# Four similarity matmuls in a row, the naming of choices behind the batch maximum's column, and the entry list ahead of the shared sums, in a decoder layer with 160 experts

## The chip, the core and the metric

The kernel runs on one core of one Trainium2 chip. The metric is the device time of one execution in microseconds (us). A core has TensorE (PE; its weight loads are shown as PEld), VectorE (DVE), ScalarE (ACT), GpSimd (POOL) and SyncE (SP). They work through their own queues of instructions and wait for each other by semaphores. Transfers run on 16 DMA engines that all queues share.

## The reference

One post-norm decoder layer on x of (4, 512, 256): self-attention with 16 heads, a two-way attention to a context of the same size, and a feed-forward part with 160 routed experts (8 per token) and one shared expert. The part that the change touches:

```python
Sim = (hc @ w1)[:, :, None] + (hq @ w2)[:, None, :] + einsum('bid,bjd->bij', hc * w3, hq) + b_sim[0]
A = softmax(Sim, axis=2)
hq_hat = einsum('bij,bjd->bid', A, hq)
Batt = softmax(max(Sim, axis=2), axis=1)
hc_bar = einsum('bi,bid->bd', Batt, hc)
hcq = concatenate([hc, hq_hat, hc * hq_hat, hc * hc_bar], -1) @ W_qv + b_qv
x2 = layernorm(x1 + hcq)
probs = sigmoid(x2 @ router_w.T + expert_bias)
top_w, top_idx = top_k(probs, 8)          # weights divided by their sum, times 2.5
out = layernorm(x2 + routed experts + shared expert)
```

## The kernel before

The layer runs in four blocks, one behind the other: `attend` (self-attention), `mix` (two-way attention, norms, routing), `experts` and `combine`. The order of every engine's work is written out by hand; there is no scheduler. The change is in `mix`.

`mix` works batch by batch (B = 4), each of 512 tokens in TT = 4 tiles of 128, in five turns n = 0 to 4. Turn n does the two-way attention of batch n (`part_b`, n < 4), the routing of batch n - 1 (`part_c`, n > 0) and the projection of batch n + 1 (`part_a`, n < 3).

In a turn, TensorE forms four tiles of similarities into PSUM banks 4, 5, 2 and 3 (`SIMILAR`), 128 x 512 each. For tile i, VectorE takes the negative row maximum (`row_max`), ScalarE the exponential with the row sums (`exp_row`), VectorE the inverse (`invert_row`), ScalarE scales (`scale_row`), TensorE transposes the row of tiles (`turn_row`, banks 6 and 7) and ScalarE copies it out (`copy_row`). With all four there, TensorE multiplies with the context (`attended(0)`, `attended(1)`). Beside this the batch's own softmax runs: `u` from the row maxima, its maximum `um` turned into one row (L1020), the global maximum `g`, spread by a matmul (L1023), then `eb`, then the sums that give `W1` (L1533). The mixing matmuls (L1057, L1063) follow.

The routing of the batch before runs through the same turn on VectorE: `highest` (8 largest of 160), `strike`, `mark` (the mask; TensorE ranks it, `rank`, L949 and L951), `name` (the indices of the eight, and their weights, written into `rows`), `count_rows` (reads the ranks), `grow`, `put` and `places`, the last two for tiles 0 and 1 and later for tiles 2 and 3. Each `places` raises `rows_done`, and POOL then scatters the rows of those tiles to the DRAM tensor `row_pool` with one indirect DMA for each tile and choice, 32 for a batch (L1985). `name` must be done before, since its results are in the rows.

In turn 4 TensorE also computes the shared expert, whose output VectorE adds for one batch at a time (`add_shared`, L1251, two additions each). `list_entries` makes the list of experts and pages; SP stores it to DRAM (L864) and loads it back for every partition (L866); `fill_tables` turns it into the tables, and `tables_done` lets SP start the weight loads of the first five entries of the experts' ring (L1593). The first row loads of the experts wait in `rows_sent` until every scatter has landed.

Of the kernel before, what the change touches and what calls it, by code (L numbers as in the profile page):

```python
# [30 lines left out]
B, S, D = 4, 512, 256  # L31
DC = D // P
TT = S // P
# [73 lines left out]
def repeated(ap, at, count):  # L107

    shape = list(ap.shape)
    return ap.unsqueeze(at).broadcast_to(shape[:at] + [count] + shape[at:])  # L110
# [504 lines left out]
class Order:  # L615
# [6 lines left out]
    def do(self, ins):  # L622
        self.n += 1
        ins.then_inc(self.sem, 1)

    def sync(self, but=0):
        self.eng.wait_ge(self.sem, self.n - but)
# [123 lines left out]
def mix(nc, inputs, opening, ps, x, ctx_t, ctx_r, od, rows, place, dispatch, last_sent, tables, w, pool, listing, pool_filled, spent):  # L751
# [8 lines left out]
    with ExitStack() as ctx:  # L760
# [149 lines left out]
        def _(pe):  # L910
# [61 lines left out]
            def step(n, part_b, part_c, part_a):  # L972
# [16 lines left out]
                def similarity(i):  # L989
                    for c in range(DC):  # L990
                        if i == 0:
                            pe.wait_ge(x1t_done, n * DC + (c + 1))
                        last = nc.tensor.matmul(ps[:, SIMILAR[i]], ET[:, c, i * P:(i + 1) * P], CT[:, c],
                                                start=c == 0, stop=c == DC - 1)
                    last.then_inc(similar, 1)

                def turn_row(i):
                    pe.wait_ge(row_scaled, tile(i))
                    if i >= 2:
                        pe.wait_ge(at_done, tile(i - 2))  # L1000
                    for j in range(TT):
                        last = nc.tensor.transpose(ps[:, 6 + i % 2, j * P:(j + 1) * P],
                                                   A[:, i, j * P:(j + 1) * P], ident)
                    last.then_inc(row_turned, 1)

                similarity(0)
                similarity(1)
                for i in range(2, TT):
                    similarity(i)
                    turn_row(i - 2)  # L1010
                if n == 0:
                    pe.wait_ge(ones_set, 3)
                    pe.wait_ge(below_set, 1)
# [67 lines left out]
                if part_a:  # L1081
                    turn_x1(n + 1)
            run(pe, start, step)

        @block.scalar
# [90 lines left out]
        def _(dve):  # L1176
# [22 lines left out]
            def step(n, part_b, part_c, part_a):  # L1199
# [33 lines left out]
                def name():  # L1233
                    for t in range(TT):
                        do(nc.vector.max_index(names8[:, t], top[:, t], pr[:, t]))
                    sync(but=TT)
                    do(nc.vector.reciprocal(winv[:], tsum[:]))
                    sync()
                    do(nc.vector.tensor_scalar(winv[:], winv[:], ROUTED_SCALE, None, ALU.mult))
                    do(nc.vector.tensor_scalar(rows[:, n - 1, :, NAMES:ROW].bitcast(I32), names8[:], -1.0, float(EXPERTS),  # L1240
                                               ALU.mult, ALU.add))
                    sync()
                    do(nc.vector.tensor_tensor(rows[:, n - 1, :, D:CODES], top[:], repeated(winv[:], 2, TOP_K), ALU.mult))
                    o2.hold()

                def add_shared(b):

                    dve.wait_ge(shared_made, b + 1)
                    shared = two(SHARES[b])
                    for t in range(0, TT, 2):  # L1250
                        last = nc.vector.tensor_tensor(XS[b][:, t:t + 2], shared[:, t:t + 2], rows[:, b, t:t + 2, 0:D], ALU.add)  # L1251
                    last.then_inc(shared_added, 1)
# [223 lines left out]
                def row_max(i):  # L1476
                    dve.wait_ge(similar, tile(i))
                    nc.vector.tensor_reduce(nmax[:, i:i + 1], ps[:, SIMILAR[i]], AX, ALU.max, negate=True).then_inc(row_maxed, 1)

                def invert_row(i):  # L1480
                    dve.wait_ge(row_expd, tile(i))
                    nc.vector.reciprocal(rinv[:, i:i + 1], rsum[:, i:i + 1]).then_inc(row_inverted, 1)
# [13 lines left out]
                if part_b:  # L1496
                    row_max(2)
                    invert_row(1)
                if part_c:
                    name()  # L1500
                if part_b:
                    row_max(3)
                    invert_row(2)
                    dve.wait_ge(row_maxed, tile(TT - 1))
                    do1(nc.vector.scalar_tensor_tensor(u[:], nmax[:], -1.0, dots[:], ALU.mult, ALU.add))
                    sync1()
                    do1(nc.vector.tensor_scalar(u[:], u[:], bsim, None, ALU.add))
                    sync1()
                    nc.vector.tensor_reduce(um[:], u[:], AX, ALU.max).then_inc(um_done, 1)
                    invert_row(3)  # L1510
                    dve.wait_ge(um_turned, n + 1)
                    nc.vector.tensor_reduce(g[:], ps[0:1, 4, 0:P], AX, ALU.max).then_inc(g_done, 1)
# [39 lines left out]
                if part_a:  # L1552
                    use_x1(n + 1)
                if part_c and not part_b:
                    add_shared(0)
                    list_entries()
                    for b in range(1, B):
                        add_shared(b)
                    fill_tables()
                    dve.sem_inc(tables_done, 1)  # L1560
            run(dve, start, step)


# [484 lines left out]
```

## Time and profile before

| | us |
|---|---|
| median of 3 runs | 868.62 (867.92 to 869.75) |
| profiled execution, whole | 870.09 |
| profiled execution, span of the core's instructions | 868.3 |
| TensorE busy in it | 742.0 (85%) |
| VectorE busy | 494.8 (57%) |
| ScalarE busy | 386.5 (45%) |
| POOL busy | 365.2 (42%) |
| mean granted clock of TensorE | 0.942 of full |

In the trace `attend` ends at about 292 us, turn 0 of `mix` starts at 294.6, turns 1 to 3 at 343.9, 394.7 and 443.4, and the first matmul of the experts at 560.6. Rows of a timeline read: start, duration, engine, line, operation, output <- input, tile shape, count of merged instructions, and in brackets the idle time of the engine before them with what ended it. A record of TensorE is half of a matmul of this type, so four records are one tile of similarities. Between 292 and 560 us no engine is busy all the time: the share of busy time says little there, and the waits in brackets say what comes last.

### The profile page before, as it was taken

The numbers are of one execution on the slowest core, as the hardware profiler recorded it, in microseconds if no ns is written. First come the engines' busy times: TensorE is split into PE (matmuls) and PEld (weight loads), VectorE is DVE, ScalarE is ACT, GpSimd is POOL, SyncE is SP. The second block draws the span as 40 slices with busy tenths as digits, with TensorE's granted clock in tenths as the row PEclk, the third lists the DMA queues.
The fourth block names the chain that finished last, engine by engine and source line by source line (L and its number), as shares of the span: only waits on it lengthen the run. The fifth ranks groups of instructions, "written<-read, shape, count | busy, mean of one in ns | idle before, by whom it ended". The sixth has DMA issues, their size and how long they took to land. (4 is left out here: it accounts for less than half of the span.)

```text
span 868.3 us, 14833 instructions
## 1 busy us (share of the span) xinstructions
PE 742.0 (85%) x3782; PEld 491.9 (57%) x3782; DVE 494.8 (57%) x1316; ACT 386.5 (45%) x809; POOL 365.2 (42%) x368
## 2 busy tenths in 40 slices
PE   7979999999999898898979730199999999998495
PEld 3645444444445366474846520188887787786373
DVE  1577787777781416768687498134333433332287
ACT  2337677676766634326171300044554454454011
POOL 9400101011100200165775777357777775777200
PEclk9999999999999999999999975599999999999698
DMA  6799878788794220042332223699999999995695
GB/s 243 261 345 303 286 250 278 259 272 276 257 297 177 63 72 25 34 170 103 131 113 74 113 99 134 224 347 374 371 380 375 368 362 347 371 345 187 259 421 218
DMA packets 103699, 208.04 MB, mean 240 GB/s; under 512 B 26024, under 2 KB 51666, under 8 KB 97377
## 3 DMA queue, kind: packets, MB, share of 16 engines
q1 hardware_dynamic: 63008, 127.39, 42.7%
q10 hardware_dynamic: 25760, 44.89, 14.7%
q0 software_dynamic: 14880, 35.17, 11.1%
q8 instruction: 22, 0.36, 0.2%
q14 instruction: 29, 0.23, 0.1%
HBM read 118.35 MB, written 96.08 MB: 247 GB/s over the span
## 5 line engine op out<-in xcount | busy, mean ns | idle before, releaser
L1831 POOL DMA_INDIRECT contributions<-c_c,e_dest x182 | 177.2, 973 | 81.1 <-ACT c_c L1809 42.0
L1985 POOL DMA_INDIRECT row_pool<-rows,places x128 | 131.2, 1025 | 121.6 <-issue 104.1
L594 DVE TENSOR_REDUCE a_mx<-ps 128x2 f32<-128x1024 f32 x128 | 151.9, 1218 | 30.3 <-PE ps L368 30.2
L539 ACT ACTIVATE a_e<-ps 128x512 f32<-128x512 f32 x256 | 135.6, 600 | 62.0 <-PE ps L398 55.8
L1783 DVE COPY e_xt<-e_psx 128x256 f32<-128x256 f32 (+1 forms) x130 | 68.6, 530 | 99.7 <-PE e_psx L1715 94.4
L1729 PE MATMUL e_psg<-e_xt,e_w 128*128 128x64 f32 (+2 forms) x676 | 118.7, 308 | 1.5 <-issue 1.1
L1715 PE MATMUL e_psx<-m_c,rows 128*128 128x128 f32 x364 | 64.8, 285 | 57.3 <-DMA rows<-row_pool 57.2
L1802 ACT ACTIVATE e_g<-e_psg 128x128 f32<-128x128 f32 (+1 forms) x130 | 41.8, 321 | 160.4 <-PE e_psg L1729 133.7
L311 POOL MEMSET a_q<- 64x1024 f32 x32 | 30.3, 946 | 179.4 <-PE ps L398 178.3
L1740 PE MATMUL e_psy<-e_w,e_g 128*128 128x256 f32 (+1 forms) x442 | 104.1, 393 | 0.0
L398 PE MATMUL ps<-a_q,a_k 128*128 128x512 f32 x256 | 98.3, 450 | 5.7 <-ACT a_e L539 3.8
L1729 PEld LDWEIGHTS e_psg<-e_xt,e_w 128*128 128x128 f32 x676 | 95.4, 194 | 5.8 <-issue 2.0
L1715 PEld LDWEIGHTS e_psx<-m_c,rows 128*128 128x128 f32 x364 | 45.2, 144 | 84.1 <-DMA rows<-row_pool 60.5
L1809 ACT ACTIVATE c_c<-e_psy,e_weight 128x256 f32<-128x256 f32 x182 | 80.5, 473 | 27.5 <-PE e_psy L1740 23.6
L398 PEld LDWEIGHTS ps<-a_q,a_k 128*128 128x128 f32 x256 | 43.8, 189 | 80.0 <-ACT a_e L539 49.3
L368 PE MATMUL ps<-a_k,a_q 128*128 128x512 f32 x256 | 86.8, 420 | 0.0
L409 PE MATMUL ps<-a_e,a_v 128*32 128x512 f32 x512 | 68.2, 605 | 0.0
L1740 PEld LDWEIGHTS e_psy<-e_w,e_g 128*128 128x128 f32 (+1 forms) x442 | 57.2, 171 | 14.4 <-ACT c_c L1809 6.3
L368 PEld LDWEIGHTS ps<-a_k,a_q 128*128 128x128 f32 x256 | 47.6, 191 | 11.1 <-issue 3.6
L1755 DVE TENSOR_TENSOR e_same<-rows,t_expert 128x56 f32<-128x56 int32 x26 | 5.6, 216 | 59.8 <-DMA rows<-row_pool 59.8
L1904 PE MATMUL c_ps<-c_c,m_c 128*128 128x256 f32 x128 | 33.2, 405 | 6.5 <-DMA c_c<-contributions 6.2
L1028 PE MATMUL ps<-m_at,m_cr 128*128 128x512 f32 x64 | 34.5, 689 | 2.7 <-ACT m_at L1127 2.7
(287 smaller groups left out, 959.9 us busy)
## 6 DMA issues: line engine op xcount, KB each, us to landing
e_w<-w ACTq DMA_DIRECT2D x162, 256.0 KB
row_pool<-fill SPq DMA_DIRECT2D x32, 1260.0 KB, 7.4
rows<-row_pool SPq DMA_DIRECT2D x139, 140.0 KB
c_c<-contributions SPq DMA_DIRECT2D x16, 1024.0 KB, 17.5
a_k<-k_parts SPq DMA_DIRECT2D x64, 128.0 KB, 3.5
rows<-row_pool SPq DMA_DIRECT2D x78, 70.0 KB
a_q<-q_parts SPq DMA_DIRECT2D x32, 128.0 KB, 4.0
a_q<-q_parts SPq DMA_DIRECT2D x64, 64.0 KB, 3.4
```

The source lines that it names most:

```text
L368: last = nc.tensor.matmul(psS[:, pair, 1 - u], Q[:, at.slot, hh, qt * P:(qt + 1) * P], K[:, at.slot, hh], start=True, stop=True)
L398: nc.tensor.matmul(psT[:, BANK[k]], K[:, at.slot, hh, kt * P:(kt + 1) * P], Q[:, at.slot, hh], start=True, stop=True).then_inc(rescored, 1)
L409: last = nc.tensor.matmul(psO[rows], V[:, at.n // NG, kt, head * 2 * DH:(head + 1) * 2 * DH], E[:, kt * HG + hh], start=kt == 0, stop=kt = ...
L539: nc.scalar.activation(E[:, i], psT[:, BANK[i]], ACT.Exp, scale=DH ** -0.5).then_inc(expd, 1)
L594: nc.vector.tensor_reduce(mx[:, at.slot, qt, 2 * DH * pair::HALF], psS[:, pair], AX, ALU.max).then_inc(maxed, 1)
L1715: last = nc.tensor.transpose(ps_x(at, (c * n + k) * P, (c * n + k + 1) * P), X[:, page(at) + k, c * P:(c + 1) * P], ident)
L1729: last = nc.tensor.matmul(ps_g(f, n)[:, k * own:(k + 1) * own], W[:, place, c * INTER:(c + 1) * INTER], XT[:, f.slot % XT_RING, at0:at0 + ...
L1740: last = nc.tensor.matmul(ps_y(f, k)[i * high:(i + 1) * high], G[:, f.slot % XT_RING, k * P + i * high:k * P + (i + 1) * high], W[:, place ...
L1783: nc.vector.tensor_copy(XT[:, at.slot % XT_RING, 0:n], ps_x(at, 0, n)).then_inc(xt_done, 1)
L1809: nc.scalar.activation(Y[:, result(f) + k], ps_y(f, k), ACT.Copy, scale=weight[:, result(f) + k:result(f) + k + 1]).then_inc(y_done, 1)
L1831: nc.gpsimd.indirect_dma_start(out=contrib, out_offset=bass.IndirectOffsetOnAxis(ap=dest[:, result(f) + k:result(f) + k + 1], axis=0), in_ ...
L1985: nc.gpsimd.indirect_dma_start(out=pool, out_offset=bass.IndirectOffsetOnAxis(ap=place[:, b, t, k:k + 1], axis=0), in_=rows[:, b, t], in_o ...
```

## The change

Three things are moved and nothing is added or taken away.

1. TensorE runs all four `similarity(i)` before the first two `turn_row(i)`. Before, similarities 0, 1 and 2 came first, then `turn_row(0)`, `similarity(3)`, `turn_row(1)`.
2. VectorE runs `name()` behind the maximum `um` and ahead of `invert_row(3)`. Before, it stood between `invert_row(1)` and `row_max(3)`. In turn 4, without a `part_b`, its place stays the same.
3. In turn 4 `list_entries()` comes before all four `add_shared(b)`. Before, `add_shared(0)` stood ahead of it.

```diff
@@ TensorE, step @@
-                similarity(0)
-                similarity(1)
-                for i in range(2, TT):
+                for i in range(TT):
                     similarity(i)
-                    turn_row(i - 2)
+                for i in range(TT - 2):
+                    turn_row(i)
@@ VectorE, step @@
                 if part_b:
                     row_max(2)
                     invert_row(1)
-                if part_c:
-                    name()
                 if part_b:
                     row_max(3)
                     invert_row(2)
...
                     nc.vector.tensor_reduce(um[:], u[:], AX, ALU.max).then_inc(um_done, 1)
+                if part_c:
+                    name()
+                if part_b:
                     invert_row(3)
                     dve.wait_ge(um_turned, n + 1)
                     nc.vector.tensor_reduce(g[:], ps[0:1, 4, 0:P], AX, ALU.max).then_inc(g_done, 1)
@@ VectorE, step, turn 4 @@
                 if part_c and not part_b:
-                    add_shared(0)
                     list_entries()
-                    for b in range(1, B):
+                    for b in range(B):
                         add_shared(b)
```

Line numbers behind the first edit are one lower in the kernel after. TensorE in turn 0, from the first similarity (`m_ct,m_et`) to `attended(0)` (`m_at,m_cr`), before:

```order
L993 MATMUL ps<-m_ct,m_et 128x512 x6
L1002 MATMUL ps<-m_c,m_a 128x128 x4
L993 MATMUL ps<-m_ct,m_et 128x512 x2
L1002 MATMUL ps<-m_c,m_a 128x128 x4
L1020 MATMUL ps<-m_c,m_um 1x128
L1002 MATMUL ps<-m_c,m_a 128x128 x4
L1023 MATMUL ps<-m_g,m_ones 128x1
L1002 MATMUL ps<-m_c,m_a 128x128 x4
L1028 MATMUL ps<-m_at,m_cr 128x512 x4
```

and after:

```order
L993 MATMUL ps<-m_ct,m_et 128x512 x8
L1002 MATMUL ps<-m_c,m_a 128x128 x8
L1019 MATMUL ps<-m_c,m_um 1x128
L1002 MATMUL ps<-m_c,m_a 128x128 x4
L1022 MATMUL ps<-m_g,m_ones 128x1
L1002 MATMUL ps<-m_c,m_a 128x128 x4
L1027 MATMUL ps<-m_at,m_cr 128x512 x4
```

The two matmuls of the fourth similarity moved ahead of the first turned row (`m_a`); in turns 1 to 3 the ranking stands between the second turned row and `m_um` in both. VectorE in turns 1 to 3, from the mask to the global maximum, before:

```order
L1230 TENSOR_TENSOR m_mask<-m_prob,m_rep 128x640
L1231 TENSOR_SCALAR m_tsum<-m_tsum 128x4
L1478 TENSOR_REDUCE m_nmax<-ps 128x1
L1482 RECIPROCAL m_rinv<-m_rsum 128x1
L1235 MAX_INDEX m_names<-m_top,m_prob 128x8 x4
...
L1243 TENSOR_TENSOR rows<-m_top,m_winv 128x4x8
L1478 TENSOR_REDUCE m_nmax<-ps 128x1
L1482 RECIPROCAL m_rinv<-m_rsum 128x1
L1505 SCALAR_TENSOR_TENSOR m_u<-m_nmax,m_dots 128x4
...
L1509 TENSOR_REDUCE m_um<-m_u 128x1
L1482 RECIPROCAL m_rinv<-m_rsum 128x1
L1512 TENSOR_REDUCE m_g<-ps 1x1
```

and after:

```order
L1477 TENSOR_REDUCE m_nmax<-ps 128x1
L1481 RECIPROCAL m_rinv<-m_rsum 128x1
L1477 TENSOR_REDUCE m_nmax<-ps 128x1
L1481 RECIPROCAL m_rinv<-m_rsum 128x1
L1502 SCALAR_TENSOR_TENSOR m_u<-m_nmax,m_dots 128x4
...
L1506 TENSOR_REDUCE m_um<-m_u 128x1
L1234 MAX_INDEX m_names<-m_top,m_prob 128x8 x4
...
L1242 TENSOR_TENSOR rows<-m_top,m_winv 128x4x8
L1481 RECIPROCAL m_rinv<-m_rsum 128x1
L1512 TENSOR_REDUCE m_g<-ps 1x1
```

The four index searches and the four small operations behind them (all of `name()`) now stand between `m_um` and the last inverse.

## Rows read from the trace of the kernel before

**Rows 1.** Timeline of POOL: scatters that had to wait, and the last.

```profile
396.06 0.97 POOL L1985 DMA_INDIRECT row_pool<-rows,places  x1 [9.38 <-ACT m_et L1101]
...
465.12 0.97 POOL L1985 DMA_INDIRECT row_pool<-rows,places  x1 [6.69 <-DVEq L1320]
...
508.58 1.02 POOL L1985 DMA_INDIRECT row_pool<-rows,places  x1 [1.14 <-DVEq L1320]
...
550.80 0.97 POOL L1985 DMA_INDIRECT row_pool<-rows,places  x1 [0.30 <-issue]
```

**Rows 2.** Timeline of TensorE in turn 1.

```profile
343.86 5.39 PE L993 MATMUL ps<-m_ct,m_et 128*128 128x512 f32 x12 [0.96 <-ACT m_et L1101]
...
351.02 0.66 PE L1002 MATMUL ps<-m_c,m_a 128*128 128x128 f32 x4 [1.77 <-ACT m_a L1123]
...
351.51 1.88 PE L993 MATMUL ps<-m_ct,m_et 128*128 128x512 f32 x4
...
354.36 0.44 PE L951 MATMUL ps<-m_mask,m_ones 128*128 128x160 bf16 x4
...
356.69 0.66 PE L1002 MATMUL ps<-m_c,m_a 128*128 128x128 f32 x4
...
358.04 5.40 PE L1028 MATMUL ps<-m_at,m_cr 128*128 128x512 f32 x8 [0.69 <-ACT m_at L1127]
```

**Rows 3.** Timeline of ScalarE in turn 1: copy 0, exponential 3, scaling 3.

```profile
352.33 0.59 ACT L1127 ACTIVATE m_at<-ps 128x512 f32<-128x512 f32 x1
...
354.16 0.69 ACT L1118 ACTIVATE m_a<-ps,m_nmax 128x512 f32<-128x512 f32 x1 [1.24 <-DVE m_nmax L1478]
...
355.93 0.71 ACT L1123 ACTIVATE m_a<-m_a,m_rinv 128x512 f32<-128x512 f32 x1
```

**Rows 4.** Timeline of VectorE in turn 1: first instruction of `name()`, maximum 3, inverse 3.

```profile
350.99 0.07 DVE L1235 MATCH_VALUE_LOAD m_names<-m_top,m_prob 128x8 f32 x1
...
353.43 0.69 DVE L1478 TENSOR_REDUCE m_nmax<-ps 128x1 f32<-128x512 f32 x1 [0.59 <-PE ps L993]
...
354.97 0.16 DVE L1482 RECIPROCAL m_rinv<-m_rsum 128x1 f32<-128x1 f32 x1 [0.19 <-ACT m_a L1118]
```

**Rows 5.** TensorE, turns 0 to 3; last a stretch (..., granted clock, DMA share, GB/s).

```profile
300.45 0.66 PE L1002 MATMUL ps<-m_c,m_a 128*128 128x128 f32 x4 [0.49 <-ACT m_a L1123]
...
365.20 3.68 PE L1028 MATMUL ps<-m_at,m_cr 128*128 128x512 f32 x8
...
408.66 3.70 PE L1028 MATMUL ps<-m_at,m_cr 128*128 128x512 f32 x8 [0.69 <-ACT m_at L1127]
...
457.62 5.36 PE L1028 MATMUL ps<-m_at,m_cr 128*128 128x512 f32 x8 [0.69 <-ACT m_at L1127]
...
360.00:362.00 2.00, 2.00 (x4) 0.73 (x3) 1.93 (x5) 0.00 (x0) 0.00 (x0) 0.50 0.00 0
```

**Rows 6.** Timeline of turn 2: `W1` on VectorE, and the first mixing matmul.

```profile
416.15 0.88 DVE L1533 SCALAR_TENSOR_TENSOR m_w<-m_wqv,m_hc 128x256 f32<-128x256 f32 x2
...
417.64 0.59 PE L1057 MATMUL ps<-m_x1b,m_c 128*128 128x256 f32 x2
```

**Rows 7.** Timeline of VectorE in turn 4: a shared sum, and the start of fill_tables.

```profile
534.68 1.28 DVE L1251 TENSOR_TENSOR m_x<-ps,rows 128x512 f32<-128x512 f32 x2
...
539.60 0.27 DVE L1446 CAST t_entry<-m_lists 128x64 int32<-128x64 f32 x1 [1.25 <-DMA m_lists<-listing]
```

**Rows 8.** SP's queue; landing of L1985's scatters; a stretch as in rows 5.

```profile
545.45 3.91 SPq L1593 DMA_DIRECT2D e_w<-w  x7
...
555.63 1.33 SPq L1604 DMA_DIRECT2D rows<-row_pool  x2
...
DMA to landing us min/median/max: 2.4/2.5/5.6
...
554.00:555.00 1.00, 0.00 (x0) 0.00 (x0) 0.00 (x0) 0.00 (x0) 0.00 (x0) 0.50 0.25 98
```

**Rows 9.** Timeline of TensorE in turn 4: the last four ranking matmuls.

```profile
497.48 0.74 PE L951 MATMUL ps<-m_mask,m_ones 128*128 128x160 bf16 x4
```

## What the change does to the time: the prediction

> **What bounds the kernel now.** I read the queue of POOL first, then worked back to what releases it. POOL sends the 128 row scatters of the routing, 32 for each batch, at a pitch of 1.28 us, and the experts cannot start before the last of them has landed [rows 1, 8]. The reader should look at the idle times in brackets. The third batch's scatters begin at 465.12 after 6.69 us of waiting for VectorE; the fourth batch's at 508.58 after 1.14 us more than the usual 0.30 gap would be, so again VectorE's release came last, with 1.14 us of slack behind it: POOL itself was free at 507.44 [rows 1]. So the end of the mixing stage is set by when VectorE publishes places in turn 4, and that by the chain of turns 0 to 3. (Turn n does the cross-attention of batch n and the routing of batch n-1.) Behind the scatters the expert stage is shifted as a whole, since all its row loads wait for them [rows 8]. One gate of POOL at 396.06 hangs on the end of turn 1 and moves with the chain [rows 1].
>
> Within a turn I then read TensorE. Similarities 0 to 2 run without a gap, 5.39 us for 12 records; then TensorE idles 1.77 us for the first scaled row, turns it, and only now runs the fourth similarity (1.88 us) [rows 2]. That late similarity is what the rest waits for: VectorE idles 0.59 us for it and takes its maximum at 353.43, ScalarE starts the last exponential at 354.16 after 1.24 us of idling, the last scaling runs at 355.93, the last row is turned at 356.69 and `attended` starts at 358.04 [rows 2 to 4]. From there on TensorE is busy without a gap up to the end of the mixing matmuls, so what is gained at 358.04 in one turn is passed to the next.
>
> **Similarity 3 ahead of the turned rows, with name() out of the way (turn 1, by its own rows).** Twelve records end at 349.25 (343.86 + 5.39). Four more at the pitch of 0.43 end at 351.0 instead of 353.39, inside the idle 1.77 us; the first turned row still starts at 351.02 [rows 2]. VectorE, with name() moved away, takes maximum 3 at 351.05 rather than 353.43, ready at 351.75. ScalarE cannot use all of these 2.4 us: it still has scaling 1 and the copy of turned row 0 ahead, which stands from 352.33 to 352.92, so exponential 3 runs at 352.8 to 353.6 rather than from 354.16 [rows 3]. Then scaling 2 (0.7) and copy 1 (0.6) fill it to 354.7.
>
> name() costs 352.84 - 350.99 = 1.85 us [rows 4]. It now starts behind the batch maximum's column, which follows maximum 3 and inverse 2 by 0.74 us: about 352.65. It ends at 354.5, and inverse 3, possible from 353.6, comes at 354.6 to 354.75. Queued behind name() are inverse 3, the global maximum `g`, count_rows and grow; scaling 3 on ScalarE and the spread matmul on TensorE wait for the first two. But ScalarE is itself not free before 354.7, so name() costs the chain at most 0.1 us. Scaling 3 runs at 354.8 instead of 355.93, the last row turns at 355.55 instead of 356.69, and `attended` starts at 356.9: **1.1 us earlier**. VectorE's own chain gains less, about 0.4 us: `g` at 354.75 and count_rows at 354.95 instead of 355.35 or so, since it holds the same work and only lost waits (0.59 for the maximum, less what it now waits for exponential 2). If ScalarE's cover were gone, name() would cost 0.9 us here (354.5 - 353.6).
>
> Turn 0 has no routing. There TensorE idles only 0.49 us ahead of turned row 0 [rows 5], so that row now goes behind 1.7 us of similarity and starts about 0.9 us later; copy 0 then sits in front of exponential 3 on ScalarE. Exponential 3 still comes 1.0 us earlier: **0.9 us**.
>
> Turn 3 is as turn 1: 1.1. Turn 2 is different, and here is what is late next: W1, which VectorE makes behind its first places, is ready at 417.03, and TensorE takes it up at 417.64 [rows 6]. With TensorE 1.1 us earlier and VectorE 0.4, the slack of 0.6 is used up: **1.0 us**. In turns 1 and 3 `attended` runs slower (below), so that slack is larger. Sum of the four turns: 0.9 + 1.1 + 1.0 + 1.1 = **4.1 us** at turn 4. The third batch's scatters start 0.9 + 1.1 + 1.0 + 0.4 = 3.4 us earlier; POOL is then free at 507.44 - 3.4 = 504.0 and VectorE releases the fourth at 508.58 - 4.1 = 504.5, so nothing is capped. The context load that SP issues after similarity 3 goes out up to 2.4 us earlier and is needed a whole turn later: nothing.
>
> **List entries ahead of the shared sums (turn 4).** One shared sum is two additions, 1.28 us as a row, 1.2 us in pitch [rows 7]. Moving the first behind the list brings the list to SP 1.2 us earlier. Its round trip through DRAM is now covered by four sums rather than three, the wait of 1.25 us ahead of fill_tables [rows 7] goes, and the tables are done 1.2 us earlier relative to the rest. That is not on the path by itself: the weight loads it releases (545.45) are through at about 554.3, long before the first expert matmul. What it can touch is the landing of the last scatter: a scatter lands in 2.5 us at the median, but the last, issued at 550.80, released the row loads only at 555.63, while seven weight loads held the DMA engines until 554.3 [rows 1, 8]. Lower bound 0 (the landing was slow for another reason), upper bound 555.6 - 550.8 - 2.5 = 2.3 us. If the scatter sits behind the loads it follows their end, 1.2 us. I take **1.0 us**, near that row. The Trainium skill, "DMA: Bandwidth & Descriptors" (its part on arbitration), says that each DMA engine goes round between its queues packet by packet. By that the scatter would not queue behind all of the loads and the gain would be nearer 0.6, the sum 0.4 us smaller; the profile's slow landing only shows that they disturb each other.
>
> **TensorE's clock, the cost that the diff doesn't show.** In turns 0, 1 and 3 the matmuls of `attended(0)` take 5.35 to 5.40 us, in turn 2 3.70, as `attended(1)` does in all four (3.68) [rows 2, 5]: the granted clock fell to 0.50 (1.2 GHz) at or just before them and they lost 1.7 us. What went before is a stretch of turned rows and small matmuls with gaps, 4.65 us long from the end of similarity 3 (353.39) to `attended` (358.04), and the same length in all four turns. The change takes 1.7 us of dense matmuls out of its front: from 351.0 to 356.9 it is 5.9 us long. Three falls in four at 4.65 us make the fourth likely at 5.9. Bounds: none of the falls (-5.1 us against now) and longer low stretches, which would catch the ranking too: its last four matmuls took 0.44 us at the full level and 0.74 in turn 4 at the low one, so its 14 would lose about 1.0 [rows 2, 9]. I take one more fall, in turn 2: **+1.7 us**.
>
> **Sum.** -4.1 - 1.0 + 1.7 = -3.4 us. Against the profiled execution (868.3 span, 870.1 with what lies around it) that is 866.7; it lies 1.5 us over the median of the timed runs, about one low-clock stretch, so that it may hold one more than a typical run. Taken from the median: 868.6 - 3.4 = **865.2 us**.
>
> **Rivals.**
> A. The clock falls as often as now: 868.6 - 5.1 = 863.5. For it: turn 2 got through 4.65 us with no fall. The Trainium skill, "TensorE: Matmul & The Clock Gate" (HAM oscillation), has the engine keep its full clock as long as it has no single long idle gap, and the change makes none; the trace disagrees, as the clock fell in turn 1 behind gaps of at most 1.8 us.
> B. The longer stretch brings the clock down before the ranking as well and in every turn: 4 x 1.7 + 3 x 1.0 = 9.8 us instead of 5.1, net -0.4: 868.2. Against it: the ranking of turn 1 still ran at the full level (0.44 us at 354.36), after that idle 1.77 us [rows 2].
> C. Slower: the same, and in two turns the low level also holds through `attended(1)`, another 1.7 us each: +3.0, 871.6. The place is the stretch in front of `attended(0)`; it decides from three more low stretches (5.1 us). For it speaks only that turn 4 shows long low stretches; against it, that `attended(0)` itself brought the clock back each time (its later part and all of `attended(1)` ran at the full level).
> D. The chain moves but POOL or the DMA takes it back: the list gains nothing, and name() in front of inverse 3 and of the places costs 0.5 us per turn, as if ScalarE had no other work ahead of scaling 3. Then -4.1 + 1.5 + 1.7 = -0.9: 867.7.
>
> **How the numbers follow.** Forecast 0.46, A 0.26 (with fewer falls than now in it), D 0.10, B 0.12, C 0.06. What can be told from no change is about 0.2% or 1.7 us: forecast and A are faster, and a third of D; B and the rest of D are the same, C slower. So faster 0.75, same 0.19, slower 0.06. The range reaches from A with 0.9 us of the list's upper bound (862.6) to B (868.2); outside are C and the rarest cases of A.
>
> **What would show it.** Right: 16 similarity records in a row; exponential 3 about 1.3 us nearer the first similarity; turned row 3 and `attended(0)` 1.1 us nearer; no idle time ahead of fill_tables; POOL's fourth batch starting 2 to 4 us earlier. Wrong on name(): ScalarE idle ahead of scaling 3 with VectorE as releaser. Wrong on the clock: `attended(0)` durations of 3.7 or over 5.4 in other turns than I said. Wrong on the list: the last scatter still takes 4.8 us until the row loads.

## The result, and the profile after

| | before | after |
|---|---|---|
| median | 868.22 us (866.27 to 869.75, 6 runs) | 861.7 us (861.31 to 864.59, 6 runs) |
| ratio | | 0.9913 [0.9888, 0.9938], or 6.5 us less |
| profiled execution, whole / span | 870.09 / 868.3 us | 861.83 / 859.7 us |
| mean granted clock | 0.942 | 0.947 |

The change gained nearly twice the 3.4 us forecast, and the time lies 0.9 us under the range. (The two profiled executions lie 8.3 us apart, since that of before is 1.9 us over its median; the medians carry the verdict, the traces the places.) The page of the kernel after, first the span, then busy time, share and count of instructions of each engine:

```profile
span 859.7 us, 14833 instructions
...
PE 739.3 (86%) x3782; PEld 490.9 (57%) x3782; DVE 494.0 (57%) x1316; ACT 386.6 (45%) x809; POOL 363.7 (42%) x368
```

The same work, only TensorE is 2.7 us less busy; two blocks less at the low clock, below, are 3.4. TensorE after, in turn 1 (answers to [rows 2]; start, duration, ..., idle time before it and its releaser), with `attended(0)` of turn 0 ahead and of turns 2 and 3 behind:

```profile
307.23 5.40 PE L1027 MATMUL ps<-m_at,m_cr 128*128 128x512 f32 x8 [0.69 <-ACT m_at L1126]
...
343.67 7.11 PE L993 MATMUL ps<-m_ct,m_et 128*128 128x512 f32 x16 [0.96 <-ACT m_et L1100]
350.83 0.66 PE L1002 MATMUL ps<-m_c,m_a 128*128 128x128 f32 x4
...
352.29 0.65 PE L1002 MATMUL ps<-m_c,m_a 128*128 128x128 f32 x4 [0.81 <-ACT m_a L1122]
...
353.47 0.44 PE L951 MATMUL ps<-m_mask,m_ones 128*128 128x160 bf16 x4
...
354.05 0.66 PE L1002 MATMUL ps<-m_c,m_a 128*128 128x128 f32 x4
...
355.23 0.66 PE L1002 MATMUL ps<-m_c,m_a 128*128 128x128 f32 x4 [0.20 <-ACT m_a L1122]
...
356.58 3.70 PE L1027 MATMUL ps<-m_at,m_cr 128*128 128x512 f32 x8 [0.69 <-ACT m_at L1126]
...
404.40 3.70 PE L1027 MATMUL ps<-m_at,m_cr 128*128 128x512 f32 x8 [0.69 <-ACT m_at L1126]
...
452.43 3.70 PE L1027 MATMUL ps<-m_at,m_cr 128*128 128x512 f32 x8 [0.69 <-ACT m_at L1126]
```

Sixteen similarity records run in a row, the idle 1.77 us ahead of the first turned row is gone, and `attended(0)` starts 12.91 us after the first similarity (356.58 - 343.67) instead of 14.18. The surprise is the duration: 3.70 us in turns 1 to 3, where [rows 2, 5] show 5.40, 3.70 and 5.36. The clock fell less often there, not more. In turn 0 nothing changed: 5.40 us after, 5.35 before.

ScalarE and VectorE after, in turn 1 (answers to [rows 3, 4]):

```profile
352.62 0.68 ACT L1117 ACTIVATE m_a<-ps,m_nmax 128x512 f32<-128x512 f32 x1
...
354.46 0.72 ACT L1122 ACTIVATE m_a<-m_a,m_rinv 128x512 f32<-128x512 f32 x1
```

```profile
350.81 0.69 DVE L1477 TENSOR_REDUCE m_nmax<-ps 128x1 f32<-128x512 f32 x1
...
352.26 0.08 DVE L1234 MATCH_VALUE_LOAD m_names<-m_top,m_prob 128x8 f32 x1
...
354.26 0.17 DVE L1481 RECIPROCAL m_rinv<-m_rsum 128x1 f32<-128x1 f32 x1
```

Exponential 3 comes 8.95 us after the first similarity instead of 10.30. Inverse 3 waits for `name()` (352.26 to 354.11) and is ready at 354.43; scaling 3 starts at 354.46 with no idle time ahead of it. ScalarE was busy up to then, so `name()` cost the chain nothing that the trace shows.

POOL, VectorE's start of fill_tables, and SP's queue after (answers to [rows 1, 7, 8]):

```profile
460.73 0.97 POOL L1984 DMA_INDIRECT row_pool<-rows,places  x1 [5.10 <-DVEq L1319]
...
502.50 1.11 POOL L1984 DMA_INDIRECT row_pool<-rows,places  x1 [0.30 <-issue]
...
544.10 0.97 POOL L1984 DMA_INDIRECT row_pool<-rows,places  x1 [0.30 <-issue]
```

```profile
532.24 0.22 DVE L1445 CAST t_entry<-m_lists 128x64 int32<-128x64 f32 x1 [0.37 <-DMA m_lists<-listing]
```

```profile
538.07 3.92 SPq L1592 DMA_DIRECT2D e_w<-w  x7
...
548.50 1.33 SPq L1603 DMA_DIRECT2D rows<-row_pool  x2
```

The fourth batch's scatters no longer wait for VectorE but for POOL itself ("issue", the usual 0.30). Before, the 1.14 us ahead of them (0.84 over that usual gap) was VectorE's.

Where the 8.60 us between the two spans went, from the starts of the same instructions:

| stretch | before | after | difference |
|---|---|---|---|
| start to first similarity of turn 0 | 294.57 | 295.28 | +0.71 |
| turn 0 to turn 1 | 49.29 | 48.39 | -0.90 |
| turn 1 to turn 2 | 50.88 | 47.91 | -2.97, of it 1.70 clock |
| turn 2 to turn 3 | 48.70 | 47.82 | -0.88 |
| turn 3 to third batch's scatters | 21.68 | 21.33 | -0.35 |
| third to fourth batch's scatters | 43.46 | 41.77 | -1.69 |
| fourth batch's to last scatter | 42.22 | 41.60 | -0.62 |
| last scatter to first row load | 4.83 | 4.40 | -0.43 |
| row load to first expert matmul | 4.96 | 4.95 | -0.01 |
| first expert matmul to end | 307.71 | 306.25 | -1.46 |

The second fall that is gone, the one of turn 3 (1.66 us), lies in the line from the third to the fourth batch's scatters. The first and last lines are not the change's: no instruction of those blocks moved, and the other profiles of either order spread over 306.7 to 309.3 us in the last one. The 32 scatters of the third batch, too, took 41.3 to 42.3 us from one trace to another, with next to nothing to wait for.

### The profile page after: what moved, and what is told of

The parts are those of the page before. It is cut to its first block and busy times, and to the rows that moved or that the text cites. A ratio compares the mean times of both kernels' runs of the same rounds, so it can differ in the third digit from the quotient of the medians.

```text
span 859.7 us, 14833 instructions
## 1 busy us (share of the span) xinstructions
PE 739.3 (86%) x3782; PEld 490.9 (57%) x3782; DVE 494.0 (57%) x1316; ACT 386.6 (45%) x809; POOL 363.7 (42%) x368
## 5 line engine op out<-in xcount | busy, mean ns | idle before, releaser
L329 PE MATMUL ps<-a_e 128*128 128x512 f32 x64 | 32.2, 645 | 4.7 <-DMA a_e<-xt 4.7
```

## Experiments: the parts by themselves

Theory: the two moves in `part_b` need each other (`name()` in its old place holds back maximum 3; moved alone, nothing covers it), and the clock's falls are the rest. Rival: the gain is one part's alone. I put each part into the kernel before.

```diff
 a_only:
-                similarity(0)
-                similarity(1)
-                for i in range(2, TT):
+                for i in range(TT):
                     similarity(i)
-                    turn_row(i - 2)
+                for i in range(TT - 2):
+                    turn_row(i)
 b_only:
-                if part_c:
-                    name()
                 if part_b:
                     row_max(3)
...
                     nc.vector.tensor_reduce(um[:], u[:], AX, ALU.max).then_inc(um_done, 1)
+                if part_c:
+                    name()
+                if part_b:
                     invert_row(3)
 c_only:
-                    add_shared(0)
                     list_entries()
-                    for b in range(1, B):
+                    for b in range(B):
 ab: a_only's and b_only's edits together
```

> Only the four similarities in a row; name() stays ahead of maximum 3. The theory of the prediction: turn 0 gains its 0.9 us, in turns 1 to 3 maximum 3 must wait for name() and comes 0.5 us earlier instead of 2.4, so attended(0) comes 0.5 us earlier: 2.4 us in all, about 866. Theory T (the clock falls in the stretch between the end of the ranking and attended(0), 3.2 us long before and 2.7 after the change): that stretch gets no shorter here, so attended(0) still takes 5.4 us in two or three turns. Rival R (the falls are a matter of chance in one execution and the change has nothing to do with them): any number of falls.

> Only name() behind the batch maximum's column; similarity 3 stays behind the first turned row. Both theories: name() (1.85 us) now stands on the way to inverse 3 with no cover, since the exponential 3 is ready at 354.8 and inverse 3 comes at 356.7: attended(0) 1.1 us later in turns 1 to 3, +3.3 us, about 871.5. Theory T: the stretch from the ranking to attended(0) grows to 4.3 us, so the clock falls in all four turns, another 1.7 us: 873. Rival R: falls as before.

> Only the list ahead of the four shared sums. If the last scatter stands behind the weight loads in the DMA queues: 1.0 to 1.2 us earlier, 867.1. If the queues take turns and the loads only slow it: 0.4 us, which is what the changed kernel showed from the last scatter to the first row load (4.83 to 4.40 us): 867.8. Wait ahead of fill_tables 1.25 us down to 0.4 or less.

> The change without its third part. All theories put nearly the whole gain here: 6.5 less 0.4 to 1.0, so 862.1 to 862.7. Theory T: attended(0) at 3.7 us in turns 1 to 3 again, since the stretch from the ranking is 2.7 us. Rival R: some of them at 5.4.

| kernel | median | ratio | `attended(0)` in turns 1 to 3 | first similarity to `attended(0)`, turns 1 to 3 |
|---|---|---|---|---|
| before | 869.7 | 1 | 5.40, 3.70, 5.36 | 14.18, 13.92, 14.18 |
| a_only | 865.38 | 0.9948 [0.9926, 0.9970] | 3.70, 5.27, 3.70 | 13.73, 13.68, 13.68 |
| b_only | 875.85 | 1.0080 [1.0056, 1.0103] | 5.20, 6.69, 5.40 | 15.15, 15.39, 15.15 |
| c_only | 868.94 | 0.9984 [0.9959, 1.0009] | 3.70, 5.31, 5.40 | not moved |
| ab | 860.94 | 0.9903 [0.9870, 0.9936] | 3.70, 3.70, 5.40 | 12.90, 12.83, 13.08 |

(Times of the row before: those run beside these four; its durations are from [rows 2, 5].)

The parts do not add: -4.3 and +6.2 us alone, -8.8 together (ab_again, the same kernel as ab, gave -5.9 us against the kernel before beside it, so that the size of the last is loose). These figures hold the clock's falls as well. By the last column alone, with the 0.94 us that a similarity moved forward gives in turn 0, a_only gains 2.1 us of the chain, b_only loses 3.4 and ab gains 4.4; the other half of a_only's 4.3 us is not the order's by that count. With `name()` in its old place, the early similarity brings 0.24 to 0.50 us per turn, less than half of what ab gains, since VectorE still names choices while the scores wait. With the similarity in its old place, `name()` costs 1.0 to 1.5 us per turn, and ScalarE shows where (b_only, turn 1):

```profile
354.43 0.16 DVE L1482 RECIPROCAL m_rinv<-m_rsum 128x1 f32<-128x1 f32 x1
...
354.62 0.72 ACT L1123 ACTIVATE m_a<-m_a,m_rinv 128x512 f32<-128x512 f32 x1 [0.86 <-DVE m_rinv L1482]
```

The 0.86 us of idling with VectorE as releaser is what the prediction named as the sign that the cover is gone. It priced that case at 0.9 us. b_only came out 6.2 us slower than the kernel before, where the order alone was expected to cost 3.3 and theory T, which put a fall in every turn, expected 1.7 more. Its order costs 3.4 us in three turns by the last column; the other 2.8 are the clock's, which was low over `attended(0)` in every turn (5.20, 6.69 and 5.40 us for 5.40, 3.70 and 5.36 are 2.8 us more) and longest in turn 2:

```profile
408.37 6.69 PE L1028 MATMUL ps<-m_at,m_cr 128*128 128x512 f32 x8 [0.69 <-ACT m_at L1127]
```

c_only can't be told from no change by its time. Its trace shows the edit doing what was said of it: the wait ahead of fill_tables falls from 1.25 us [rows 7] to 0.39.

```profile
541.71 0.22 DVE L1446 CAST t_entry<-m_lists 128x64 int32<-128x64 f32 x1 [0.39 <-DMA m_lists<-listing]
```

## Experiments: what the clock's falls cost

The prediction's step "three falls in four at 4.65 us make the fourth likely" had the wrong sign, so two questions follow: what do the falls cost, and what decides them? For the first I gave TensorE two matmuls with the identity in time in which it idles anyway, behind the turned `um` and behind the last turned row. They write a bank that `attended(0)` overwrites, and add nothing to the output.

```diff
 before_fill, after_fill:
                 nc.tensor.transpose(ps[0:1, 4, 0:P], um[:], ident).then_inc(um_turned, 1)
+                nc.tensor.matmul(ps[:, 2, 0:2 * P], ident, ET[:, 0, 0:2 * P], start=True, stop=True)
...
                 turn_row(TT - 1)
+                nc.tensor.matmul(ps[:, 2, 0:2 * P], ident, ET[:, 0, 0:2 * P], start=True, stop=True)
```

For the second, theory T: what counts is the time from the ranking to `attended(0)`. It was 4.2 to 4.4 us in b_only, which fell everywhere, and 2.7 us in the change's turn 1. rank_early moves the ranking forward in the changed kernel and stretches that time to 4.1 to 4.3 us with nothing else moved; T wants the falls back.

```diff
 rank_early, against the changed kernel:
-                for i in range(TT - 2):
-                    turn_row(i)
+                turn_row(0)
...
                 if part_c:
                     pe.wait_ge(row_expd, tile(1))
                     rank(n)
+                turn_row(1)
```

> The kernel before with two dense matmuls more in each turn, 128x256 each, 0.43 us, put into TensorE's idle time: one behind the batch maximum's column (idle 0.5 us follows), one behind the last turned row (idle 0.69 us follows). Their result is overwritten and not used. Theory T (sparse TensorE between the ranking and attended(0) lets the clock fall, each fall costs 1.7 us, and the changed kernel gains from having fewer): attended(0) stays at 3.7 us in turns 1 to 3, the fillers cost at most 0.3 us a turn, so 1.5 to 4 us faster than before: 866 to 868. Rival R (the falls come from elsewhere, or cost nothing at the end since POOL binds): same as before or up to 1 us slower, 869 to 871.

> The changed kernel with the same two fillers. Theory T: few falls are left to remove in turns 1 to 3, so within 1 us of the changed kernel, and closer to before_fill than the changed kernel is to the kernel before: the difference between the two filled kernels is the 4.5 us of the reordering alone, plus 0.4 of the list. Rival R: the difference stays at the whole 6.5 to 8 us.

> The changed kernel with the ranking one place earlier, between the first and the second turned row. The critical chain has room for it: turned row 1 goes back by 0.3 us behind 0.8 us of idle time. Only the sparse stretch from the ranking to attended(0) grows, from 2.7 to about 4.0 us. Theory T: the clock falls ahead of attended(0) in most of turns 1 to 3, +2 to +5 us against the changed kernel, 864 to 867. Rival R: the same as the changed kernel within 1 us.

> The changed kernel itself, for a second profile and for its time on the same chip as the three others. Theory T: attended(0) again at 3.7 us in at least two of turns 1 to 3. Rival R: as often at 5.4 as in the kernel before (two of three).

| kernel | median | ratio | `attended(0)` at 3.70 in turns 1 to 3 |
|---|---|---|---|
| before, beside them | 869.01 | 1 | |
| before_fill | 865.02 | 0.9952 [0.9932, 0.9972] | 3 of 3 |
| after_fill | 862.40 | 0.9916 [0.9899, 0.9934] | 3 of 3 |
| after_again (the change) | 862.61 | 0.9925 [0.9909, 0.9942] | 3 of 3 |
| rank_early | 861.36 | 0.9912 [0.9891, 0.9934] | 3 of 3 |

Added work made the old order 4.0 us faster. In before_fill, turns 1 and 2:

```profile
357.00 3.70 PE L1030 MATMUL ps<-m_at,m_cr 128*128 128x512 f32 x8 [0.25 <-ACT m_at L1129]
...
405.91 3.70 PE L1030 MATMUL ps<-m_at,m_cr 128*128 128x512 f32 x8 [0.25 <-ACT m_at L1129]
```

From one `attended(0)` to the next it is 48.91 us (405.91 - 357.00). In the kernel before it is 50.62 us over a fall (358.04 to 408.66) and 48.96 over none (408.66 to 457.62) [rows 2, 5]. So a fall is worth 1.7 us of the chain, and the fillers themselves cost nothing. With no fall from turn 1 to turn 3 on either side, the order alone can be read: 48.91 and 48.96 us per turn in before_fill, 47.84 and 48.01 in after_fill, **1.07 and 0.95 us** in the two turns. From the start of turn 1 to the third batch's scatters it is 119.55 against 117.07 us, 2.5 us; with turn 0's 0.94 that makes 3.4, the prediction's figure. The medians of the two differ by 2.6 us. The low level is not gone from them, though: in turn 0 it lay over the similarities in both traces, 1.7 us over the full level in before_fill and 3.0 in after_fill.

```profile
293.48 7.08 PE L993 MATMUL ps<-m_ct,m_et 128*128 128x512 f32 x12 [2.24 <-PEq L179]
```

```profile
293.73 10.12 PE L993 MATMUL ps<-m_ct,m_et 128*128 128x512 f32 x16 [2.39 <-PEq L179]
```

And the same two fillers gave the changed kernel nothing that can be measured: 862.40 us with them, 862.61 (after_again) without.

rank_early kept all three `attended(0)` at the full level:

```profile
349.60 0.44 PE L951 MATMUL ps<-m_mask,m_ones 128*128 128x160 bf16 x4
...
354.16 3.70 PE L1027 MATMUL ps<-m_at,m_cr 128*128 128x512 f32 x8 [0.69 <-ACT m_at L1126]
```

The ranking ends at 350.04, 4.12 us ahead of `attended(0)`, and nothing fell. Theory T, as a matter of that time alone, is out.

## Experiments: how often it falls, and how far fillers go

Falls differ from one execution to another of the same kernel, so I repeated both kernels (after_third, before_again) and ab, and put two more fillers at the end of the self-attention block. There TensorE idles 2.2 to 2.4 us at the change of blocks, and in 7 of the 17 traces without these two fillers the low level then lay over the similarities of turn 0, where 12 records at the full level take 5.39 us, as in [rows 2]. In c_only:

```profile
294.77 8.40 PE L993 MATMUL ps<-m_ct,m_et 128*128 128x512 f32 x12 [2.39 <-PEq L179]
```

A second theory, S, stood for what is left: the order inside the turn decides.

```diff
 after_fill_all: after_fill, and behind the last step of attend
+            nc.tensor.matmul(psT[:, 0], ident[:], E[:, 0], start=True, stop=True)
+            nc.tensor.matmul(psT[:, 0, 0:2 * P], ident[:], E[:, 0, 0:2 * P], start=True, stop=True)
```

> The changed kernel with the two fillers of each turn and two dense matmuls more (128x512 and 128x256, 1.3 us) at the end of the self-attention block, where TensorE idles 2.4 us until the first similarity of turn 0. In five of ten profiles so far the clock was low over the similarities of turn 0 (12 records in 8.4 instead of 5.4 us). Theory T (a fall is brought on by sparse TensorE work ahead of it, and costs the end time): no low stretch left between 292 and 480 us, 1 to 2 us faster than the changed kernel, about 861. Rival R (falls at the change of blocks come from something else): the same as the changed kernel or slower by the 0.3 us by which the block change may be delayed.

> The change without its third part, on the same chip as the whole change and in more rounds. If the list is worth 0.4 us (the landing of the last scatter, 4.83 to 4.40 us): 0.4 us slower than the changed kernel. If it is worth the 1.0 us of the prediction: 1.0 slower. If nothing: the same.

> The changed kernel itself, in more rounds beside the two others, and for a third profile. 6.4 us faster than the kernel before. Theory T: at most one of turns 1 to 3 with attended(0) at 5.4 us. Rival R: two, as in the kernel before.

> The kernel before itself, for a second profile. Theory T: two or three of the four turns with attended(0) at 5.4 us. Rival R: any number, so one or none is as likely.

| kernel | median | ratio | `attended(0)`, turns 0 to 3 |
|---|---|---|---|
| before, beside them | 868.67 | 1 | |
| before_again | 869.61 | 1.0008 [0.9987, 1.0029] | 5.29, 5.40, 3.70, 5.36 |
| after_third | 861.22 | 0.9908 [0.9881, 0.9935] | 5.26, 3.70, 3.70, 3.70 |
| ab_again | 862.82 | 0.9924 [0.9897, 0.9950] | all 3.70 |
| after_fill_all | **859.89** | 0.9889 [0.9865, 0.9914] | all 3.70 |

The kernel before falls again in turns 1 and 3 (before_again):

```profile
358.50 5.40 PE L1028 MATMUL ps<-m_at,m_cr 128*128 128x512 f32 x8 [0.69 <-ACT m_at L1127]
...
409.10 3.70 PE L1028 MATMUL ps<-m_at,m_cr 128*128 128x512 f32 x8 [0.69 <-ACT m_at L1127]
...
458.06 5.36 PE L1028 MATMUL ps<-m_at,m_cr 128*128 128x512 f32 x8 [0.69 <-ACT m_at L1127]
```

after_fill_all has the lowest median of all kernels run: 859.26 to 860.96 us over six executions, with 860.22 to 864.61 for the change on the same chip. The two ratios' intervals overlap, so its 1.3 us over the change is likely and not settled. Its one trace has the two fillers, the similarities of turn 0 at the full level, and a granted clock of 1.00 across the change of blocks (stretch: bounds, length, busy PE, PEld, DVE, ACT, POOL, granted clock, DMA share, GB/s):

```profile
292.32 1.02 PE L496 MATMUL ps<-a_e,a_ident 128*128 128x512 f32 x2
...
294.72 7.11 PE L995 MATMUL ps<-m_ct,m_et 128*128 128x512 f32 x16 [0.94 <-PEq L179]
```

```profile
292.00:300.00 8.00, 7.06 (x21) 3.35 (x21) 5.10 (x14) 4.16 (x10) 4.55 (x11) 1.00 0.46 149
```

The idle time there is 0.94 us instead of 2.24 to 2.39, and the similarities take 7.11 us for 16 records, as in turn 1. The timed executions say much the same of the whole kernel: time at the low level, worked out as (1 - granted clock) x 2 x span and averaged over each kernel's executions, is 99 to 101 us before, 93 to 94 after, 91 in before_fill, 87 in after_fill_all, 91 to 92 in ab and ab_again, and 107 in b_only. after_fill doesn't fit: 96 us over its four executions (93 to 100), more than the change without fillers.

## Experiments: order or length of the turn

The new order also makes the turn one us shorter, so the falls could hang on the turn's length (theory L) and not on the order (S). I lengthened both with matmuls behind `attended(1)`, where TensorE has no slack: the change by three (49.0 to 49.3 us per turn, the old length without a fall), the kernel before by five (51.1 to 51.4, over the old length with one).

```diff
 after_pad (3 times), before_pad (5 times):
                 attended(1)
+                for _ in range(3):
+                    nc.tensor.matmul(ps[:, 6, 0:2 * P], ident, ET[:, 0, 0:2 * P], start=True, stop=True)
```

> The changed kernel with three dense matmuls more (128x256, 1.3 us together) behind attended(1) of each turn 0 to 3, far from the stretch ahead of attended(0). A turn then takes 49.2 us from first similarity to first similarity, as one without a fall does in the kernel before, instead of 47.9. Theory S (it is the order of the work ahead of attended(0) that keeps the clock up): attended(0) at 3.7 us in turns 1 to 3, time + 3.9 us (three turns ahead of the third batch's scatters) against the changed kernel, 866. Theory L (what keeps it up is when a turn's sparse stretch comes round, that is the length of a turn): one or two of turns 1 to 3 at 5.4 us, + 5 to 7 us, 867 to 869.

> The same kernel as after_pad, for a second profile and more timed executions; the theories expect of it what they expect there.

> The kernel before with five such matmuls (2.1 us) behind attended(1) of each turn, so that a turn without a fall takes 51.3 instead of 49.2 us. The work ahead of attended(0) is untouched. Theory S: two of turns 1 to 3 at 5.4 us as before, + 6.4 us, about 876. Theory L: other turns fall, or fewer do: at most one of turns 1 to 3, + 3 to 4.5 us, 872 to 873.5.

> The same kernel as before_pad, for a second profile and more timed executions; the theories expect of it what they expect there.

| kernel | median | ratio | falls, turns 1 to 3 |
|---|---|---|---|
| after_pad | 866.33 | 0.9971 [0.9950, 0.9991] | 0 of 3 |
| after_pad_2 | 866.69 | 0.9974 [0.9950, 0.9998] | 0 of 3 |
| before_pad | 876.22 | 1.0086 [1.0059, 1.0113] | 0 of 3 |
| before_pad_2 | 875.23 | 1.0088 [1.0060, 1.0116] | 0 of 3 |

after_pad in turn 1, then before_pad in turn 1:

```profile
357.07 3.70 PE L1027 MATMUL ps<-m_at,m_cr 128*128 128x512 f32 x8 [0.69 <-ACT m_at L1128]
```

```profile
359.01 3.70 PE L1028 MATMUL ps<-m_at,m_cr 128*128 128x512 f32 x8 [0.69 <-ACT m_at L1129]
```

The first pair says: the new order holds the clock at the old length too, against L. The second says: the old order, made longer still by dense work, doesn't fall either, against S as the only cause. The padding itself is dense work, so it is no pure change of length; that wasn't taken apart. The price of before_pad was mis-stated as well: five matmuls in four turns are 4 x 2.15 = 8.6 us, and the two runs came out 6.6 and 5.7 us slower than the kernel before beside them (869.58). The 2.0 to 2.9 us between are somewhat less than two falls of 1.7, which its traces no longer have in turns 1 and 3.

All traces together, slow `attended(0)` in turns 1 to 3: old order (before, before_again, c_only) 6 of 9; b_only 3 of 3; a_only 1 of 3; new order (after, after_again, after_third, ab, ab_again, rank_early) 1 of 18; padded 0 of 12; filled 0 of 9. That the new order falls less is a count of these executions, and it holds for turns 1 to 3. In turn 0 `attended(0)` was slow in all three traces of the change (5.25 to 5.40 us), in rank_early and in after_pad_2, but not in ab and ab_again; in before and before_again it was slow as well.

One reading of the traces orders most of the counts. Add up TensorE's idle times in brackets from a turn's first similarity to `attended(0)`, in turns 1 to 3: 4.0 to 4.2 us in b_only (3 of 3 slow), 2.7 to 3.0 in the old order (6 of 9), 2.3 to 2.5 in a_only (1 of 3), 1.7 to 1.9 in the new order (1 of 18), 1.1 to 2.0 with fillers (0 of 9). Against it as the only cause stand the padded old order, with 3.0 us and none slow in 6, and turn 0 of the change, slow with 1.7. No run varied this time by itself without adding or moving work, so why the new order falls less stays open.

## Why the prediction was wrong, point by point

**The reordering was right.** `attended(0)` came 0.94, 1.27, 1.10 and 1.15 us nearer to the first similarity in turns 0 to 3, for 0.9, 1.1, 1.0 and 1.1 forecast. The filled pair gives 1.07 and 0.95 us per turn with the clock out of it, and 3.4 us up to the third batch's scatters, the figure of the prediction. Its step for `name()` ("costs the chain at most 0.1 us") held in the change, and b_only shows the 0.9 us that it named for ScalarE without cover.

**What is late next: right about W1, wrong about POOL.** The first mixing matmul starts 3.64 us behind the start of `attended(1)` in turn 2 and 3.79 in turn 3, for 3.52 in turn 2 before (from 414.12 to 417.64 [rows 6]): 0.12 and 0.27 us of waiting for `W1`. The prediction read POOL's 1.14 us as coming on top of the usual 0.30; it is the whole idle time, so the slack was 0.84. That alone would have capped nothing (504.3 against its 504.5). "So nothing is capped" failed, because the clock gave VectorE more than was forecast: it published the fourth batch's places 6.5 us earlier (500.87 for 507.39), POOL came free only 5.2 us earlier (502.2 for 507.44). The scatters start 502.50, where VectorE's lead as before (1.19 us from the start of that instruction to the scatter) would have had them at 502.06: 0.4 us capped. VectorE's publishing instruction after:

```profile
500.87 0.17 DVE L1316 TENSOR_SCALAR places<-m_k 128x16 uint32<-128x16 f32 x1
```

**The clock: the step that failed.** "I take one more fall, in turn 2: +1.7 us" should have read two fewer in the chain: `attended(0)` took 3.70 us in each of turns 1 to 3, and 5.40 in turn 0 only. The step took the span from similarity 3 to `attended(0)` as what decides, from one trace with three falls and one non-fall at the same length; four observations that do not vary in the cause can't show it. The change made that span longer (5.9 us planned, 5.8 in turn 1) and the falls of turns 1 to 3 ceased in all three of its traces. Of the 6.5 us, about 3.4 to 3.8 are by estimate the reordering with the list, and some 3 the clock. The medians split it the other way: the fillers, which took the falls from `attended(0)`, gave the kernel before 4.0 us, ratio 0.9952 [0.9932, 0.9972], and the order on top of them 2.6. The runs don't settle which. Rival A (fewer falls than now included) was the right one, and the range gave it too little room: it held A with the falls of before, not A with two of them gone. The Trainium skill, "TensorE: Matmul & The Clock Gate" (HAM oscillation), asks for one long idle gap before the clock goes down. The traces disagree: those of the kernel before and of b_only, with 5.40 and 6.69 us for `attended(0)` behind gaps of at most 1.8 us in the turn, and that of the change in turn 0, with 5.40 us behind gaps of at most 0.69 us since the first similarity.

**The list: right mechanism, too large.** It was put at 1.0 us. From the last scatter to the first row load it is 4.23 us on average over the nine traces with the early list (3.62 to 4.47) and 4.65 over the nine with the late one (3.75 to 5.28): about 0.4 us, with an overlap wider than the difference. c_only's ratio (0.9984 [0.9959, 1.0009]) and ab against the change don't resolve it. In the change the weight loads go out 6.0 us ahead of the last scatter instead of 5.4, so the step's "1.2 us earlier relative to the rest" was 0.7; with the late list that lead varied by itself, from 4.7 us in b_only to 6.7 in ab_again. Of the two readings in the prediction, the one by the Trainium skill, "DMA: Bandwidth & Descriptors" (arbitration), at 0.6 us was nearer than the one by the row at 1.2.

**What the range left out.** It was built with the falls of one execution as if they were a property of the kernel, and the bound that its own clock step gave (none of the falls, -5.1 us) never entered it. They vary: in ab, whose order in turns 0 to 3 is the change's, one trace shows a fall in turn 3 and the other (ab_again) none.

## What to carry to other kernels

Where TensorE's matmuls after a stretch of small ones last longer than the same matmuls elsewhere, measure that first: put dense matmuls with a harmless result into the idle time, and see what the stage is worth at the full level. Here that gave the old order 4.0 us for two added lines, and the new order nothing. Two moves that only pay together must be costed together: each needs the other's cover. And of a clock effect seen in one trace of one kernel, neither its sign nor its size should carry a sum; take a second trace, or give both signs a place in the range.

## What the runs showed of the hardware

- The granted clock falls in the midst of work that never pauses for more than 1.8 us (for 0.69 us in turn 0 of the change), and each fall costs the next dense block 1.7 us (eight records in 5.40 us instead of 3.70, the granted clock 0.50, so 1.2 GHz, in the stretch of [rows 5]); in b_only one cost 3.0 us (6.69).
- Added dense work in idle time made a kernel faster: 869.01 to 865.02 us with two 128x256 matmuls per turn. In the kernel whose `attended(0)` was at the full level in turns 1 to 3 already, it changed nothing (862.61 and 862.40).
- The same kernel's falls differ from execution to execution. The low time averaged over timed executions separates the kernel before (99 to 101 us) from the change (93 to 94) and b_only (107), but not every pair: after_fill has 96.
- One idle stretch of 2.4 us between blocks had the first 12 records of the next take 8.40 us instead of 5.39 (c_only); with dense work in it and 0.94 us of it left, in one trace, they ran at the full level. In the trace of the change the same idle time, 2.39 us, was followed by 16 records at the full level (7.10 us), so that idle time alone doesn't decide it; 7 of 17 traces with 2.2 to 2.4 us of it show the low level there.
- POOL's indirect scatters go at 0.97 us and 0.30 of issue, but now and then one takes up to 1.6 us, so that the third batch's 32 vary by 1.0 us.
